# Projecting context and z rows through the output weights before the attention weighs them

## What is computed

```
z      = layernorm(x)
q      = z @ wq.T ;  k_new = z @ wk.T ;  v_new = z @ wv.T
k      = concat(context, k_new) ;  v = concat(context, v_new)
attn   = softmax(q @ k.T / 16)
x      = x + tanh(g_xattn[0]) * ((attn @ v) @ wo.T)
```

## Time and profile before

| | |
|---|---|
| median of 3 runs | 811.12 us (810.39 to 813.89) |
| span of the profiled execution | 806.8 us |
| PE busy | 741.4 us, 92% |
| DVE busy | 633.1 us, 78% |
| ACT, POOL busy | 384.9 us (48%), 398.0 us (49%) |
| mean granted clock of PE | 0.975 |
| one full turn (scores to scores) | 88.9 us |

### The profile page before, as it was taken

The page is one execution under the profiler, slowest core; times in us unless marked ns, Lnnn a source line. Parts: engine busy times, 40 slices in busy tenths (PEclk is TensorE's granted clock), DMA queues, the critical chain, the costliest instruction groups (busy, mean ns, idle before and its releaser), DMA issues.

```text
span 806.8 us, 13118 instructions
## 1 busy us (share of the span) xinstructions
PE 741.4 (92%) x4582; PEld 642.7 (80%) x4582; DVE 633.1 (78%) x1043; ACT 384.9 (48%) x730; POOL 398.0 (49%) x382
## 2 busy tenths in 40 slices
PE   6988799889999999989998999989998999968896
PEld 5876687778888788878887888878887988746785
DVE  2857589687978798888989798888979797899532
ACT  3536434556355644654455645653465635431321
POOL 1024332364746365464636465455546464565364
PEclk8999979999999999999999999999999999988999
DMA  8170002010022013110032113110121000101121
GB/s 249 53 208 1 1 1 53 27 54 27 27 79 67 27 38 81 45 47 13 26 78 66 35 30 78 55 37 26 43 74 53 26 26 26 41 26 40 34 73 51
DMA packets 35895, 41.19 MB, mean 51 GB/s; under 512 B 3118, under 2 KB 27096, under 8 KB 35864
## 3 DMA queue, kind: packets, MB, share of 16 engines
q1 hardware_dynamic: 35864, 40.78, 17.6%
HBM read 36.45 MB, written 4.33 MB: 51 GB/s over the span
## 4 chain that ended last, share of the span: by engine, by line
PE 59%; DVE 15%; issue 4%; POOL 3%; ACT 1%; DMA 1%; DVEq 0%; POOLq 0%; ACTq 0%
PE sums L475 14%; PE gate_ps L475 13%; PE up_ps L475 12%; PE transit L475 6%; DVE wk L1389 3%; DVE wk L1394 3%; PE transit L540 3%; PE transit L467 3%; PE transit L552 3%; DVE wk L1396 2%; POOL act_sb L1139 2%; PE transit L520 1%; POOL hid_l L1130 1%; DVE act_sb L1379 1%; DVE za_l L1333 1%
## 5 line engine op out<-in xcount | busy, mean ns | idle before, releaser
L1130 POOL TENSOR_TENSOR hid_l<-act_sb,hid_h 128x512 fp32r<-128x512 f32 (+1 forms) x128 | 173.3, 1354 | 171.9 <-ACT hid_h L917 171.9
L917 ACT ACTIVATE hid_h<-act_sb 128x512 fp32r<-128x512 f32 (+1 forms) x128 | 80.4, 628 | 150.9 <-POOL act_sb L1139 117.8
L1139 POOL TENSOR_TENSOR act_sb<-act_sb,late 128x512 f32<-128x512 f32 x64 | 92.0, 1438 | 100.2 <-DVE act_sb L1381 80.9
L1379 DVE SCALAR_TENSOR_TENSOR act_sb<-act_sb,gate_ps 128x512 f32<-128x512 f32 (+1 forms) x128 | 85.8, 670 | 68.9 <-ACT act_sb L901 68.9
L475 PE MATMUL sums<-down_h,hid_h 128*128 128x256 f32 x320 | 92.3, 288 | 12.7 <-POOL hid_l L1130 12.7
L475 PE MATMUL sums<-down_h,hid_l 128*128 128x256 f32 x320 | 90.0, 281 | 0.0
L475 PE MATMUL sums<-down_l,hid_h 128*128 128x256 f32 x320 | 90.0, 281 | 0.0
L1381 DVE TENSOR_TENSOR act_sb<-act_sb,up_ps 128x512 f32<-128x512 f32 x120 | 82.4, 687 | 4.1
L901 ACT ACTIVATE act_sb<-gate_ps 128x512 f32<-128x512 f32 x80 | 47.2, 590 | 71.4 <-PE up_ps L475 66.1
L475 PEld LDWEIGHTS sums<-down_h,hid_h 128*128 128x128 f32 x320 | 60.9, 190 | 19.8 <-issue 17.9
L475 PE MATMUL gate_ps<-zm_h,gate_h 128*128 128x512 f32 x140 | 62.3, 445 | 5.6 <-DVE act_sb L1381 5.6
(11 more groups left out here) (194 smaller groups left out, 1962.7 us busy)
## 6 DMA issues: line engine op xcount, KB each, us to landing
late<-combine_rows SPq DMA_DIRECT2D x64, 256.0 KB, 3.2
ctx_tok<-in_ctx SPq DMA_DIRECT2D x8, 512.0 KB, 4.9
vals<-in_ctx SPq DMA_DIRECT2D x16, 256.0 KB, 5.6
out_x<-late SPq DMA_DIRECT2D x8, 512.0 KB, 3.2
xa<-in_x SPq DMA_DIRECT2D x7, 512.0 KB, 3.5
wk<-in_L_ffn_w SPq DMA_DIRECT2D x2, 682.0 KB
late<-in_L_ffn_w_down SPq DMA_DIRECT2D x1, 1024.0 KB, 6.6
wk<-in_L_ffn_w_gate SPq DMA_DIRECT2D x2, 512.0 KB, 4.4
```

The lines of the kernel that those rows point to most:

```text
L917: nc.scalar.activation(hid_h[0:n, pos], act_sb[0:n, pos], ACT.Copy).then_inc(hid_h_set, 1)
L1130: nc.gpsimd.tensor_tensor(hid_l[0:n, pos], act_sb[0:n, pos], hid_h[0:n, pos].bitcast(F32), ALU.subtract).then_inc(hid_l_set, 1)
L1139: nc.gpsimd.tensor_tensor(act_sb[:, pos], act_sb[:, pos], comb_sb[:, pos], ALU.mult).then_inc(weighted, 1)
L1379: nc.vector.scalar_tensor_tensor(mine, mine, 1.0, gate_ps[pos][0:hidden_rows(chunk)], ALU.add, ALU.mult).then_inc(gated_one, 1)
```

## The change

The product of probabilities and rows, followed by the product with `wo`, is turned round: the rows of `vals` are multiplied by `wo` first, and the probabilities then weigh projected rows, straight to the sum that DVE adds to x.

- v rows: once at the start, PE transposes the raw `wv` (`turn_wv`), ACT copies it (`keep_wv`), and PE multiplies it by `wo` (`fuse_wv_wo`) into a bank of PSUM. High and low parts of `wv` are then taken from that product, so `values` (its instructions unchanged) gives v already projected. The load of `wo` moves ahead of the first context load, and ACT's high part of `wv` moves behind the first `normalise`.
- context rows: a new step `context_out` on PE, in every turn of stage A, multiplies the transposed context in `keys` by `wo` (per block 16 fp32 matmuls, 64 columns stationary, 256 moving, halves of output partitions alternating) into two new uses of the banks, u0 and u1; ACT copies them to `vals` in four copies of 64 partitions. It stands right behind `values`: before `m_down(3)` and `scores` in the full turns, before `scores` in turn 1. The two transfers of context rows into `vals` go.
- `attend` becomes 8 matmuls per block (probabilities of one sequence stationary, 64 columns; 256 moving) into wo0 and wo1. `project`, the uses oT0 and oT1, ACT's two copies of them and two fillers `keep_clock(3)` go; in turn 0 `keep_clock(10)` becomes `fuse_wv_wo` and `keep_clock(4)`.

The code of DVE and POOL is not changed.

```diff
@@ -29,13 +29,13 @@
     ("A", "ctxT0"), ("A", "ctxT1"), ("M", "combT"), ("W", "z2T0"), ("W", "z2T1"), ("A", "z0T0"), ("A", "z0T1"),
-    ("A", "q0"), ("A", "q1"), ("A", "k0"), ("A", "k1"), ("A", "v0"), ("A", "v1"), ("A", "scores"), ("A", "pT"),
-    ("A", "oT0"), ("A", "oT1"), ("A", "wo0"), ("A", "wo1"), ("A", "z1T0"), ("A", "z1T1"), ("W", "yT0"), ("W", "yT1"),
+    ("A", "q0"), ("A", "q1"), ("A", "k0"), ("A", "k1"), ("A", "v0"), ("A", "v1"), ("A", "u0"), ("A", "u1"),
+    ("A", "scores"), ("A", "pT"), ("A", "wo0"), ("A", "wo1"), ("A", "z1T0"), ("A", "z1T1"), ("W", "yT0"), ("W", "yT1"),
...
@@ -356,7 +356,11 @@
+        raw_wv = raw_qkv[:, 2 * KH * D:].rearrange("p (k e) -> p k e", k=KH)
+        wv_turned = x2[:, 0:KH]
+        parts["wv"] = (up_ps[0][:],) + parts["wv"][1:]
-        loaded = {"wq": (qkv_in[0], 16), "wk": (qkv_in[1], 16), "wv": (qkv_in[2], 16), "route": (route_in, 16),
+        loaded = {"wq": (qkv_in[0], 16), "wk": (qkv_in[1], 16), "wv": (fuse_done, 1), "route": (route_in, 16),
...
@@ -366,8 +370,9 @@
+                sp.dma_start(wo[:], woT.rearrange("(k p) e -> p k e", p=P)).then_inc(wo_in, 16)
 
             def other_weights():
...
-                sp.dma_start(wo[:], woT.rearrange("(k p) e -> p k e", p=P)).then_inc(wo_in, 16)
...
-                    sp.dma_start(vals[S:P, :, 0], ctx_seqs[t.i, 0]).then_inc(ctx_val_in, 16)
-                    sp.dma_start(vals[0:S, :, 1], ctx_seqs[t.i, 1]).then_inc(ctx_val_in, 16)
...
@@ -511,6 +513,34 @@
+            def turn_wv():
+                pe.wait_ge(qkv_in[2], 16)
+                for m in range(KH):
+                    for k in range(KH):
+                        last = nc.tensor.transpose(gate_ps[0][:, m * D + k * P:m * D + (k + 1) * P], raw_wv[:, k, m * P:(m + 1) * P], ident[:])
+                last.then_inc(fuse_turned, 1)
+
+            def fuse_wv_wo():
+                pe.wait_ge(fuse_kept, 1)
+                pe.wait_ge(wo_in, 16)
+                for k in range(KH):
+                    for m in range(KH):
+                        last = nc.tensor.matmul(up_ps[0][:, k * D:(k + 1) * D], wv_turned[:, m, k * P:(k + 1) * P], wo[:, m],
+                                                start=m == 0, stop=m == KH - 1)
+                last.then_inc(fuse_done, 1)
+
+            def context_out(t):
+
+                wait_taken(pe, t, "A", "ctxT0", "ctxT1", claims=("A", "u0"))
+                for pair in range(2):
+                    bank, full = claim(t, "A", f"u{pair}")
+                    for r in range(2):
+                        for k in range(KH):
+                            for q in range(2):
+                                last = nc.tensor.matmul(bank[(1 - q) * S:(2 - q) * S, r * D:(r + 1) * D], keys[:, k, 2 * pair + r, 1 + q],
+                                                        wo[:, k], start=k == 0, stop=k == KH - 1)
+                    last.then_inc(full, 1)
...
@@ -530,27 +560,15 @@
             def attend(t):
...
-                    bank, full = claim(t, "A", f"oT{h}")
-                    for r in range(NT):
-                        for q in range(2):
-                            cols = slice((2 * r + q) * S, (2 * r + q + 1) * S)
-                            last = nc.tensor.matmul(bank[:, cols], vals[:, r, q, h * P:(h + 1) * P], probsT[:, cols],
-                                                    start=True, stop=True)
...
-            def project(t):
...
-                        for k in range(KH):
-                            last = nc.tensor.matmul(bank[:, r * D:(r + 1) * D], qo[:, k, (2 * pair + r) * P:(2 * pair + r + 1) * P],
-                                                    wo[:, k], start=k == 0, stop=k == KH - 1)
+                        for q in range(2):
+                            tile = 2 * pair + r
+                            cols = slice((2 * tile + q) * S, (2 * tile + q + 1) * S)
+                            last = nc.tensor.matmul(bank[q * S:(q + 1) * S, r * D:(r + 1) * D], probsT[:, cols], vals[:, tile, q],
+                                                    start=True, stop=True)
...
@@ -652,6 +670,7 @@
                     keep_clock(12)
+                    turn_wv()
                 context_T(t)
...
                 if first:
-                    keep_clock(10)
+                    fuse_wv_wo()
+                    keep_clock(4)
                 z_T(t, "A", "z0T", za_row, 1)
...
                 q_and_k(t)
                 values(t)
+                context_out(t)
                 m_down(3)
                 scores(t)
...
                 attend(t)
                 m_up(6)
-                if first:
-                    keep_clock(3)
-                project(t)
                 m_up(7)
...
@@ -865,10 +882,18 @@
-            def attend(t):
-                for h in range(KH):
-                    bank = wait_full(act, t, "A", f"oT{h}")
-                    nc.scalar.activation(qo[:, h], bank[:], ACT.Copy).then_inc(free_of("A", f"oT{h}"), 1)
+            def keep_wv():
+                act.wait_ge(fuse_turned, 1)
+                nc.scalar.activation(wv_turned, gate_ps[0][:].rearrange("p (m e) -> p m e", m=KH), ACT.Copy).then_inc(fuse_kept, 1)
+
+            def context_out(t):
+                for pair in range(2):
+                    bank = wait_full(act, t, "A", f"u{pair}")
+                    for q in range(2):
+                        half = slice((1 - q) * S, (2 - q) * S)
+                        last = nc.scalar.activation(vals[half, 2 * pair:2 * pair + 2, q],
+                                                    bank[half].rearrange("p (r d) -> p r d", r=2), ACT.Copy)
+                    last.then_inc(free_of("A", f"u{pair}"), 1)
...
@@ -935,8 +960,9 @@
-                    for name in ("wq", "wk", "wv"):
-                        high(name)
+                    high("wq")
+                    high("wk")
+                    keep_wv()
...
                 normalise(t, "A", 1, xa, za_row, rstd_a, shift_a)
+                if first:
+                    high("wv")
                 m_chunk(3)
...
                 values(t)
+                context_out(t)
                 if first:
...
                 probs_T(t)
                 if w:
                     readouts(t, 1)
-                attend(t)
...
@@ -1019,13 +1047,13 @@
                 k_wide(t)
+                context_out(t)
                 softmax(t)
                 probs_T(t)
                 for h in range(KH):
                     decays(t, h)
-                readouts(t, 0)
-                attend(t)
-                readouts(t, 1)
+                for h in range(KH):
+                    readouts(t, h)
```

More of the change, by code:

```diff
@@ L37 @@
 SECOND = [("A", "z0T0"), ("A", "z0T1"), ("A", "q0"), ("A", "q1"), ("A", "k0"), ("A", "k1"), ("A", "v0"), ("A", "v1"),
-          ("A", "ctxT0"), ("A", "ctxT1"), ("W", "z2T0"), ("W", "z2T1")] + TRANSIT[TRANSIT.index(("A", "scores")):]
+          ("A", "ctxT0"), ("A", "ctxT1"), ("W", "z2T0"), ("W", "z2T1"), ("A", "u0"), ("A", "u1")] + TRANSIT[TRANSIT.index(("A", "scores")):]
 CHUNKS = [("M", c) for c in range(10)] + [("A", c) for c in range(6)]
@@ L532, in attend @@
             def attend(t):
-                wait_taken(pe, t, "A", "v0", "v1", "pT", claims=("A", "oT0"))
-                pe.wait_ge(ctx_val_in, t.count("A", 32, 32))
-                for h in range(KH):
-                    bank, full = claim(t, "A", f"oT{h}")
-                    for r in range(NT):
-                        for q in range(2):
-                            cols = slice((2 * r + q) * S, (2 * r + q + 1) * S)
-                            last = nc.tensor.matmul(bank[:, cols], vals[:, r, q, h * P:(h + 1) * P], probsT[:, cols],
-                                                    start=True, stop=True)
-                    last.then_inc(full, 1)
-            def project(t):
-                wait_taken(pe, t, "A", "oT0", "oT1", claims=("A", "wo0"))
-                if t.fixed and t.i == 0:
-                    pe.wait_ge(wo_in, 16)
+                wait_taken(pe, t, "A", "v0", "v1", "u0", "u1", "pT", claims=("A", "wo0"))
                 for pair in range(2):
```

6 lines of the change are left out of this document (3 added, 3 removed).

## The result

The change makes the kernel slower: 853.57 us (four runs, 850.30 to 859.58) beside 812.5 us for the kernel before on the same chip (810.39 to 813.90), a ratio of 1.051 with a 95% interval of 1.048 to 1.055. That is 41.1 us; the spans of the two profiled executions, 850.5 and 806.8, differ by 43.7, because the one of before lies 5.7 under the median of its runs and the one of after 3.1.

A forecast was written before the change was run, and what follows sets the result against it. Bound: PE and an equally long path from scores through DVE's row maximum to z1T. 806.8 + 28.9 (full turns) + 6.1 (turn 0) + 1.2 (turn 1) + 5.1 (clock) = 848.1; with 4.3 for the runs' median, 852 us, range 836 to 864.

The forecast's parts named there:

- The path: Full turns: scores through DVE's row maximum to z1T has fixed length; late scores delay z1T, PE savings behind them hide nothing.
- The full turns, 28.9: Scores 4.82 us late in each of six turns: 1.27 wait for v0's copy, 3.45 context_out, 0.1 change of form.
- rival 3: context_out's two halves of 256 moving columns don't run side by side: 28 us more, 880; 7%.
- scores to z1T still 25.0: Full turns: the stretch from scores to z1T keeps its 25.0 us after the change.
- Rival 2: DVE's and POOL's long operations get short in the new alignment, partly absorbing the delay: 834, anything from 817 to 838; 8%.
- The clock, 5.1: PE's bunched waits ahead of z1T lower its clock, 1.7 us a fall, in half of six turns; bounds 0 and 10.2.
- Turn 1, 1.2: context_out before scores: 0.2 us not hidden, plus 0.9 for z1T's transposes at lower clock; 0 to 4.
- Turn 0, 6.1: Scores 6.1 us late: z0T 2.4 late from 16 passes for wv's product, then context_out 3.45 and 0.2; bounds 4.5 and 8.
- Rival 1: PE's passes decide, so only its savings of 1.4 us a block count: 11 us, giving 800; 3%.
- rival 4: Nothing is moved that counts, delay and savings cancel: 811 within 0.5%; 2%.

The follow-up runs named there:

- e3: Kernel before with one of the two contractions of project left out (8 records fewer per block); 810.43 us, ratio 1.000.
- e1: Kernel after with context_out, and ACT's copies of u, moved behind probs_T; 812.47 us, ratio 1.002.
- e13: Kernel before with m_up(5) of the full turns computed twice into the same banks; 827.7 us, ratio 1.018.
- e2: Kernel after with ACT's high part of chunk 5 held back until DVE's first add_now is done; 852.35 us, ratio 1.051.
- e11: Kernel after with m_up(8) of the full turns computed twice into the same banks; 853.52 us, ratio 1.052.
- e5: e1 with scores ahead of m_down(3), ACT's copies to vals ahead of the readouts, row_max between the halves' scans; 810.96 us, ratio 1.001.
- e6: Kernel after with m_down(3) put between values and context_out in the full turns; 852.07 us, ratio 1.051.
- e7: Kernel after with one of context_out's two contractions left out (16 records instead of 32); 851.72 us, ratio 1.053.
- e10: e1 with scores, m_up(5), m_down(3) in order, m_up(6) before m_down(4), copies to vals before readouts, row_max between second-half scans; 805.66 us, ratio 0.995.
- e9: e6 with m_up(8) of the full turns also computed twice into the same banks; 845.27 us, ratio 1.045.

## Why the prediction was right

The time predicted, 852, is 1.6 off the median of 853.57, and the direction, the main path and its price were right. The sum itself was right partly by luck, because two errors cancel.

- **The path.** DVE idle ahead of the row maximum: 4.9 predicted, 4.80 measured, with PE's scores as its end. That PE's saving hides nothing is shown by e3 and e1. It was incomplete that only the scores were named as the start: m_up(5) ends at the same gate and is put back by context_out just as much (in the kernel after its tanh even waits 0.54 for it, 0.22 before). The number is the same, but the sentence that work behind the scores hides nothing needs the limit that e13 shows: only behind m_up(5).
- **The full turns, 28.9.** From values to gate(5) it was 29.4, 4.90 a turn against 4.82: 1.19 of wait beyond the usual step of 0.12 (1.27 predicted) and 3.60 from context_out's first start to the next instruction's (3.55), the rest in the first step of m_down(3), 0.22 (383.81 to 384.03) where 0.12 is usual. The 32 records are 0.106 apart on average, 3.29 from first to last: two start 0.01 apart, the next two 0.21 later. The pairs are there, and rival 3 falls. From the last pair (383.50) to m_down(3) it is 0.31, 0.10 more than from pair to pair. The Trainium skill (TensorEngine Tiling (Array Packing), Key Properties) has the engine drained at a change of tiling mode; by the rows that is the 0.1 here that the prediction took, less than the whole record of 0.28 that I had weighed for it.
- **The step that failed: scores to z1T still 25.0.** It is 26.12. The prediction called ACT's copies of oT off the path and let them go at no price, and let DVE's operations only keep their length or get shorter. The copies had kept POOL's low part of chunk 5 off `add_now`; without them the two meet, 1.1 us a turn, 6.7 in all. e2 shows this, with 25.0 again. Rival 2 had the right mechanism with the wrong sign.
- **The clock, 5.1.** 4.7 in the intervals between full turns, three of five. Where PE waits was seen rightly (about 2.4 ahead of z1T predicted, 2.47 from start to start). But I read a fall off the length of one wait, between 2.17 and 2.47, and that does not hold: the clock fell behind waits of 1.93 and 1.98 and stayed up behind 2.31 to 2.38. That half of the turns would pay was a guess, and that it came out is luck.
- **Turn 1, 1.2.** 1.2 measured, but not by its steps: context_out ran partly at the lower clock, from 94.83 to the scores at 99.54 (4.7, with 3.4 counted), the row maximum waited 1.08, and z1T lost nothing beyond that (from z1T of turn 0 on, both are 1.2 later).
- **Turn 0, 6.1.** The term that was mis-sized most. Only 0.28 appears in these two executions. From values to z1T it is 27.74 instead of 24.60: 3.1, where 3.7 was counted for context_out. The other 2.4, ahead of z0T, are not there. I counted 16 passes for wv's product; it is four matmuls, eight records:

```profile
11.02 1.89 PE L528 MATMUL up_ps<-wo,x 128*128 128x256 f32 x8
```

  They cost 1.89 at the full clock (3.62 at the lower one in e11), in place of 12 filler records. From the first transposes of the context to the last value record it is 14.96 in e3, without the change's start, and 14.92 to 14.97 in the five executions with it whose clock, like that of e3, stayed up there (after, e5, e6, e7, e10): the new start adds nothing. The kernel before took 15.92 for this, with the clock low from 8.6 to 15.5, and began it at 11.95, when its context had landed; the kernel after began at 10.09. These 2.86 hide most of the 3.1, and they are the chance of two executions: the beginning lies between 9.95 and 11.95 in the five executions without the change's start, and between 9.38 and 11.14 in the nine with it.

So 6.7 missing in the full turns stand against 5.8 too many in turn 0, about half of which is chance. Rival 1 falls by e3; rival 4 by the time.

## What to carry to other kernels

Work put into a hand-written order is priced by its place: the same 3.6 us of matmuls in each turn cost 41 us ahead of the point where two paths meet, with the wait, the collision and the falls of the clock that came with that place, and nothing measurable behind it; and a trade of engine time for engine time says nothing until that point is found. A wait's named releaser shows one of the paths only; doubling a step on the other (here m_up(5)) tells whether it has slack. And a copy that goes may have kept two other engines apart, so that what it lets come earlier has to be followed as well.

## What the hardware showed

- **DVE beside POOL.** An addition of 128x512 takes DVE 0.68 us alone and 1.78 beside POOL's subtraction, which itself goes from 1.27 to 1.75. The 22 DVE operations of this form that took over 1 us in the kernel after (16 in the one before) all began while POOL was at work, and all ended 0.54 to 0.55 us after POOL's instruction did. The six more are all at the first operation of `add_now` (L1454 13 times, L1426 7). The Trainium skill (SBUF — State Buffer, Who interferes with whom) says that a DVE instruction with two SBUF inputs contends with a GpSimd instruction that reads SBUF, and that the later one blocks until the other is through. The rows agree for both: DVE's addition started at 396.10 with POOL at work until 397.33, and ends at 397.88; POOL's subtraction had itself started later, at 395.58, than a DVE operation that ran until 396.17.
- **One program's time moves with its granted clock.** e9 ran from 842.82 us at a mean granted clock of 0.974 to 853.94 at 0.955, e7 from 847.60 at 0.966 to 856.40 at 0.951. Gains of 1.1 to 1.4 us a turn in e2, e6 and e7 were given back to it in the profiled executions, as the table's third column shows.
- **Halves side by side.** A record of 64 stationary and 256 moving columns of fp32, in alternating halves, costs 0.106 on average; a record with 128 stationary columns 0.216.
